# Layer 0 of an eight-layer kernel as one order of steps: attention of later groups, weight making and feed-forward on five engines

## What is computed

```
x = x + _layernorm(_L0_attn_ref(_layernorm(x), Wq, bq, Wk, bk, Wv, bv))
x = x + _layernorm(_L0_ffn_ref(_layernorm(x), gate_w, gate_su, gate_sv, up_w, ..., down_sv))

# attention: for each token alone, 16 queries, 16 keys and 16 values (the 32 heads' queries are summed)
scores = einsum('bsdh,bse->bsde', q, k) * scale;  o = einsum('bsde,bse->bsd', softmax(scores), v)
# feed-forward, 512 -> 1792 -> 512, every weight made from a rank-4 product:
w_eff = w * (su @ sv);  a = x @ gate_eff.T;  b = x @ up_eff.T;  y = (silu(a) * b) @ down_eff.T
```

## Time and profile before

| | us |
|---|---|
| median of 3 runs | 4261.45 |
| lowest and highest | 4254.96, 4264.74 |
| span of the profiled execution | 4243.4 |
| first stage of layer 0 | 0 to 187.9 |
| feed-forward of layer 0 | 187.9 to about 640 |

### The profile page before, as it was taken

How to read it: one execution, slowest core, us unless ns; L and a number is a source line. 1 busy time by engine, 2 the same in 40 slices (tenths; PEclk the granted TensorE clock), 3 DMA queues, 4 the chain that set the end, 5 groups by cost and what they waited for, 6 DMA issues and landing times.

```text
span 4243.4 us, 63398 instructions
## 1 busy us (share of the span) xinstructions
PE 3775.5 (89%) x21648; PEld 1876.8 (44%) x21648; DVE 2793.0 (66%) x4541; ACT 2277.0 (54%) x3947; POOL 1888.5 (45%) x1566
## 2 busy tenths in 40 slices
PE   6799998899888779999999999999999985867899
PEld 2344443223322245555555555555555542443344
DVE  6633235774675468888888888988888866566322
ACT  5522223555456556676666667666676644453222
POOL 5500000000000347787786878777787774462000
PEclk9999997889889989999999999999999997998999
DMA  3100001001100010000000000000000010012100
GB/s 110 54 6 1 0 12 34 1 1 18 35 7 4 10 42 1 24 12 25 13 14 24 1 25 13 25 13 19 18 1 27 4 37 27 23 46 73 31 10 20
DMA packets 62821, 91.36 MB, mean 22 GB/s; under 512 B 12357, under 2 KB 36440, under 8 KB 62500
## 3 DMA queue, kind: packets, MB, share of 16 engines
q1 hardware_dynamic: 61832, 86.72, 7.2%
q10 hardware_dynamic: 672, 0.59, 0.1%
HBM read 73.62 MB, written 6.85 MB: 19 GB/s over the span
## 4 chain that ended last, share of the span: by engine, by line
PE 65%; DVE 15%; issue 8%; ACT 6%; POOL 4%; DMA 1%; SPq 1%; DVEq 0%; POOLq 0%; ACTq 0%
PE psum L329 14%; PE psum L330 14%; PE psum L331 14%; PE psum L1396 3%; DVE arena L1558 3%; PE psum L2499 2%; PE psum L2503 2%; PE psum L1369 2%; PE psum L2491 2%; PE psum L2460 2%; PE psum L1380 2%; ACT xn L218 1%; DVE x L2185 1%; PE psum L2482 1%; PE psum L1365 1%
## 5 line engine op out<-in xcount | busy, mean ns | idle before, releaser
L329 PE MATMUL psum<-xt_hi,arena 128*128 128x512 f16 (+2 forms) x2272 | 872.7, 384 | 31.4 <-DVE arena L531 10.8
L330 PE MATMUL psum<-xt_lo,arena 128*128 128x512 f16 (+2 forms) x2272 | 872.0, 384 | 0.0
L331 PE MATMUL psum<-xt_hi,arena 128*128 128x512 f16 (+2 forms) x2272 | 871.0, 383 | 0.0
L2286 POOL TENSOR_TENSOR arena<-arena 128x1024 f16<-128x1024 f16 x256 | 514.5, 2029 | 50.3 <-DVE arena L2097 33.5
L1314 POOL TENSOR_TENSOR rs<-sd,epsc 128x1 f32<-128x1 f32 x15 | 8.2, 548 | 1087.5 <-DVE sd L1606 1087.5
L329 PE MATMUL psum<-arena 128*128 128x512 f16 (+1 forms) x1152 | 422.4, 370 | 58.3 <-DVE arena L2914 19.0
L1509 ACT ACTIVATE arena<-psum 128x512 f32<-128x512 f32 x576 | 319.7, 598 | 266.3 <-PE psum L1380 176.7
L1558 DVE TENSOR_REDUCE arena<-psum 128x1 f32<-128x512 f32 (+3 forms) x608 | 365.1, 654 | 148.1 <-PE psum L1369 147.1
L330 PE MATMUL psum<-arena 128*128 128x512 f16 (+1 forms) x1152 | 422.2, 370 | 0.0
L331 PE MATMUL psum<-arena 128*128 128x512 f16 (+1 forms) x1152 | 422.1, 370 | 0.0
L329 PEld LDWEIGHTS psum<-xt_hi,arena 128*128 128x128 f16 (+1 forms) x2272 | 224.6, 99 | 280.9 <-issue 16.0
(11 more groups left out here) (338 smaller groups left out, 7882.1 us busy)
## 6 DMA issues: line engine op xcount, KB each, us to landing
arena<-m_wi SPq DMA_DIRECT2D x64, 320.0 KB, 3.0
arena<-m_wo SPq DMA_DIRECT2D x32, 256.0 KB, 2.6
arena<-arena SPq DMA_DIRECT2D x90, 64.0 KB, 2.5
x<-L_attn_x SPq DMA_DIRECT2D x4, 1024.0 KB, 8.3
out<-x SPq DMA_DIRECT2D x4, 1024.0 KB, 4.3
arena<-gate_wT SPq DMA_DIRECT2D x16, 224.0 KB, 2.5
arena<-up_wT SPq DMA_DIRECT2D x16, 224.0 KB, 2.5
arena<-down_wT SPq DMA_DIRECT2D x14, 256.0 KB, 2.6
```

What stands on the lines that cost most here:

```text
L329: nc.tensor.matmul(out, lh, rh, start=start, stop=False)
L330: nc.tensor.matmul(out, lh, rl, start=False, stop=False)
L331: return nc.tensor.matmul(out, ll, rh, start=False, stop=stop)
L2286: nc.gpsimd.tensor_tensor(m4_ar[:, q], heads[q].broadcast_to([P, HG, P]), m4_le.unsqueeze(1).broadcast_to([P, HG, P]), ALU.mult).then_inc( ...
```

## The change

Both stages become one `STEPS0`, walked by `sp_l0`, `pe_l0`, `act_l0`, `dve_l0` and `pool_l0`. Ahead of group 0's products stand only its attention, its "ln" tiles, group 1's "x0" tiles and 16 piece steps. The other 30 piece steps stand two by two after the up products of group 0. The attention of group g+1, its "ln" tiles and the "x0" tiles of group g+2 stand among the blocks of group g; groups 1 to 3 are straight code now. The pieces go by column block (all of gate and up for one fourth of the columns, then the next), and gate f of group 0 waits for the pieces of its own column block. Statistics, scale and power are made for four tiles at once; the square root of these norms is a power on POOL, no longer on ACT. POOL has three `raw1` buffers and multiplies in place. The rank product takes one f16 matmul over 76 rows: rows 0 to 11 hold high x high, 32 to 43 high x low, 64 to 75 low x high of the factors of gate, up and down. For that DVE clears the factor tiles, SP loads each factor three times ahead of all pieces, ACT and DVE convert them. Layer 1's four weight planes are made beside group 1. Not shown: new addresses in the arena, which grows from 34213 to 38100 words of a partition, and a smaller scratch for DMA descriptors.

```diff
-        SEQ0 = [("x0", i) for i in range(3 * GT)]
-        for i in range(GT):
-            SEQ0 += [("ln", i), ("x0", 3 * GT + i)]
-        SEQ0 += [("ln", i) for i in range(GT, NT)]
...
+        for c in range(4):
             for k in range(KT):
-                for c in range(4):
+                for m, (h_, l_) in enumerate(((gh, gl), (uh, ul))):
...
+        def block1(f):
+
+            return 2 * KT * (((f + 1) * P - 1) // QW + 1)
...
+                def batch(n, f):
+                    add(after, f, *[("stat", n + j) for j in range(GT)], ("var", n))
+                    add(after, f + 1, ("scale", n), ("norm", n), ("norm", n + 1))
+                    for j in range(GT):
+                        add(before, f + 2 + j, ("tr", n + j))
+                        add(after, f + 2 + j, ("hi", n + j), ("lo", n + j))
+                        if j + 2 < GT:
+                            add(after, f + 2 + j, ("norm", n + j + 2))
+                if g + 1 < NG:
+                    add(after, 1, ("qkv", g + 1))
+                    for q, part in enumerate(ATTN0[1:]):
+                        add(after, 2 + q, (part, g + 1))
+                    batch(entry0("ln", (g + 1) * GT), 8)
+                if g + 2 < NG:
+                    batch(entry0("x0", (g + 2) * GT), 2)
+                for f in range(F0):
+                    steps.append(("gate", g, f))
+                    if g and f == 1:
+                        steps.append(("carry", g - 1))
+                    steps.extend(before.get(f, []))
+                    steps.append(("up", g, f))
+                    chunk(2)
+                    steps.extend(after.get(f, []))
+                steps.append(("hidden", g))
+                chunk(len(chunks))
+                steps += [("tile", g, j) for j in range(GT)]
...
+            load_x(sp, 0)
+            sp.wait_ge(w1_made, 2)
+            for m, (wide, narrow) in enumerate((("gate_suT", "gate_sv"), ("up_suT", "up_sv"), ("down_sv", "down_suT"))):
+                for part in range(3):
+                    rows = slice(32 * part + RANK * m, 32 * part + RANK * (m + 1))
+                    sp.dma_start(fac_w[rows, :], A[wide]).then_inc(w1_fac, 16)
+                    sp.dma_start(fac_n[rows, m, :], A[narrow]).then_inc(w1_fac, 16)
...
                     if n >= 2:
-                        pe.wait_ge(xt_ok, n - 1)
+                        pe.wait_ge(xt_ok, n - 1 if n < 2 * GT else n)
...
-                nc.tensor.matmul(ps_y[:, i % 2, 0:w], svT[0:RANK, k * P:(k + 1) * P], suT[0:RANK, cols],
+                nc.tensor.matmul(ps_y[:, i % 2, 0:w], fac_nh[0:FR, m, k * P:(k + 1) * P], fac_wh[0:FR, cols],
                                  start=True, stop=True).then_inc(w1_ps, 1)
...
+            for what, n, *f in STEPS0:
+                if what == "factors":
+                    dve.wait_ge(w1_made, 4)
+                    nc.vector.scalar_tensor_tensor(out=fac_wh[64:FR, :], in0=fac_w[64:FR, :], scalar=WS, in1=fac_wh[64:FR, :],
```

More of the change, by code:

```diff
@@ L1090, in pe_front, with pe_l0 @@
+        def pe_l0(pe):
             pe.wait_ge(consts_ok, 5)
-            for what, n in STEPS0:
+            for what, n, *f in STEPS0:
                 if what == "tr":
@@ L1114, in pe_front, with pe_l0_block @@
                             rank(pe, i)
+                elif what in ("gate", "up"):
+                    pe_l0_block(pe, what, n, *f)
+                elif what == "carry":
+                    Tail.pe_x(pe, entry0("tail", n * GT + GT - 1), GT - 1)
+                elif what == "tile":
+                    g, j = n, f[0]
+                    r = g * GT + j
+                    if r >= 2:
+                        pe.wait_ge(y_norm, r - 1)
+                    tok = slice(j * P, (j + 1) * P)
+                    for f in range(F0):
+                        if j == 0:
+                            pe.wait_ge(hid_lo, g * F0 + f + 1)
+                            if g == 0:
+                                if f == 0:
+                                    pe.wait_ge(w1_rk, len(chunks))
+                                pe.wait_ge(w1_lo, GATED1 + f + 1)
+                        last = three(pe, ps_y[:, j % 2, :], hid_h[:, f, tok], hid_l[:, f, tok], dh[:, f, :], dl[:, f, :],
+                                     f == 0, f == F0 - 1)
+                    last.then_inc(y_ready, 1)
+                    if j:
+                        Tail.pe_x(pe, entry0("tail", r - 1), j - 1)
+        def pe_l0_block(pe, what, g, f):
+            i, cols, fc = g * F0 + f, slice(g * GW, (g + 1) * GW), slice(f * P, (f + 1) * P)
+            bank = 2 * (f % 2) + (what == "up")
+            high, low = (gh, gl) if what == "gate" else (uh, ul)
+            if what == "gate":
+                if f == 0:
+                    pe.wait_ge(xt_ok, entry0("ln", g * GT) + GT)
+                if f >= 2:
+                    pe.wait_ge(hid_ok, i - 1)
+                if g == 0:
+                    pe.wait_ge(w1_lo, block1(f))
+            for k in range(KT):
+                last = three(pe, ps_g[:, bank, :], high[:, k, fc], low[:, k, fc], xt_hi[:, k, cols], xt_lo[:, k, cols],
+                             k == 0, k == KT - 1)
+            last.then_inc(gate_ready if what == "gate" else up_ready, 1)
         def rank(pe, i):
@@ L1147, in act_front @@
                     act.wait_ge(a0_w, 2)
[L1148 removed]
+                    nc.scalar.activation(w0h, w0, ACT.Copy, scale=WS).then_inc(a0_w, 1)
                 elif what == "logits":
```

381 lines of the change are left out of this document (247 added, 134 removed).

## The result

The changed kernel takes **4209.65 us** (median of four runs, 4201.33 to 4215.07) against 4258.2 for the kernel before in the same comparison (4250.86 to 4264.74): a ratio of 0.9883, 95% interval 0.9865 to 0.9901, or 48.6 us less. The forecast was 43 us less. The profiled execution spans 4207.6 us and was timed at 4209.37, so only 1.8 us lie around a span.

What follows compares the result with a forecast made beforehand. PE bounds the feed-forward groups (100% busy); the 187.9 us stage ahead is held by small pieces handed round in strict order. 102 - 22 - 16 - 14 - 1 - 6 = 43 us off 4261.5 gives 4218 us, range 4200 to 4238.

Steps and rivals of the forecast that it cites:

- Front, 86 us: Layer 0 ahead of the products: first product at 86 us instead of 187.9, a gain of 102 us.
- New work, 22 us: Rank products, transposes and small matmuls added on PE beside layer 0's products: 22 us (18 to 30).
- Waits, 31 us: PE's waits among layer 0's products: 16 us in group 0, 14 in group 1, 1 in group 2.
- rank 24: Group 0: PE waits for a rank copy standing behind ACT's delayed silu of block 3, 2.8 us.
- tile 15: Group 0: this tile's transposes wait behind DVE's four additions, 8.0 us against 3.0, so 5.0.
- closing: End of group 0: PE waits for the last rank copy before the down products, 3.0 us.
- Clock, 6 us: Groups 0 and 1: granted clock drops at long PE waits, costing 6 us (0 to 12).
- four of my waits are that long: Groups 0 and 1: waits of 2.8 with 2.2, 5.0, 5.6 and 3.5 each cost about 1.5 us of clock.
- The 18 us: Whole kernel before: median about 18 us above the profiled span, carried over unchanged.
- R1: Beside the products: waits mostly vanish as DVE and ACT run ahead, front done at 80; 4186 us, chance 0.22.
- R2: Groups 0 and 1: nine or so waits each drop the clock, 15 + 12 instead of 6; 4239 us, chance 0.20.
- R3: Group 0: the ring of pieces sets the pace, a loss above 4.8 us a piece, 4282 at 5.5; chance 0.08.

Runs made afterwards that it cites:

- experiment 2: Changed kernel with group 0's statistics, norms, planes and small matmuls ahead of the factor conversion, and attention weights loaded before the factors; 4201.8 us, ratio 0.9864.
- experiment 5: Changed kernel with the edits of experiment 1 and experiment 2, plus group 1's x load issued on SP before its first wait for a piece; 4190.09 us.
- experiment 4: Changed kernel with each f16 rank product issued four times; one run, 4205.44 us.
- experiment 1: Changed kernel with high part, low part and next norm ahead of the attention's weights, means and addition in blocks 4 to 7, groups 0 and 1; 4184.32 us.
- experiment 9: Kernel before, unchanged, profiled a second time; span 4248.8 us, layer 0 ending at 631.87.
- experiment 7: Changed kernel with the old piece order, all gate pieces then all up pieces, so 33 piece steps precede the products; one run, 4224.14 us.

## Why the prediction was right

**Front, 86 us: right, in part by luck.** Its steps came where they were forecast. The factors landed at 13.65 us (15.5 forecast), the first statistics began at 21.88 ("near 23"), the first norm at 28.70 ("near 29"), the first additions ended at 68.1 (69) and the first product came at 85.81.

```profile
13.65 1.28 ACT L1236 ACT_TABLE_LOAD   x1 [13.65 <-DMA arena<-down_suT]
...
21.88 0.69 DVE L1320 BATCH_NORM_STATS2 arena<-x 128x6 f32<-128x512 f32 x1
```

Within the first of them four terms were off and about cancelled, which is luck: an issue of a factor took 0.34 us from one to the next, not 0.50, so eighteen cost 6.1 us instead of 9.0; the last factor landed 3.5 us after its issue (10.12 to 13.65), not 2.5; ACT had a table load of 1.28 ahead of its conversions; POOL's power of four columns took 1.03 us, not the 0.55 of one column. What the forecast did not see is that its chain had another beside it of nearly the same length: the statistics at 22 us were on it, yet experiment 2 took them off and gained nothing, because x was late as well and, as far as experiment 5 shows, the pieces.

**New work, 22 us: right.** In group 0 it is 34.2 us (145.4 less 111.2) less 15.7 of waits and 7.1 of clock (0.06 of 118.2), 11.4, where the terms that fall there (31 rank products 6, eight sets of transposes 4, one of small matmuls 2) make 12. There are 29 rank products, not 31, by the order of steps; at the 0.20 us of experiment 4 that is still 6. The 0.2 us was an estimate, and no run shows a rank product's price among dense products by itself: the 0.22 of the earlier trace rows belongs to an f16 matmul of 512 columns, and experiment 4's 0.20 is worked out from group 0's time, waits and clock. The f32 product of before took 1.86 us (x2) in the old front, which are one piece and not two, since line 1124 has 64 records for its 32 pieces. In group 1 it is 21.4 - 10.7 - 5.1 (0.04 of 127) = 5.6, forecast 6; in group 2, 3.0, forecast 4. Together 20.0. These are remainders: an error of 0.6 us in either clock term, from the rounding of the column, would stand in them.

**Waits, 31 us: 26.4.** Place by place, forecast and measured: rank 24 2.8 and 3.08; tile 12 2.2 and 0.52; tile 13 2.1 and 1.88; tile 14 0.8 and 1.62; tile 15 5.0 and 4.37; closing 3.0 and 2.69 with 0.47; one of 1.07 before the second batch was not forecast. Sum 15.7 against 16. Group 1: 5.6 and 4.37, 3.2 and 2.37, 1.2 and 0.33, 3.5 and 2.79, 0.7 and 0.79: 10.65 against 14. Group 2 had none. The walk through DVE's order named the places, and came out 0.7 to 1.2 us too high on each of group 1's first four; whether its gaps between DVE's steps or the product's end were too pessimistic was not tested. For tile 15 the additions were the mis-sized part, 4.17 us and not the 5.5 taken from the earlier trace rows.

**Clock, 6 us: the step that was too small.** The windows give 7.1 and 5.1, 12 us, the upper end of 0 to 12. What failed is less the price than the count. "About 1.5 us each" is near the 1.7 of a single fall (the earlier trace rows have the 0.43 only at the start of the products; behind the wait that ended at 146.86 seven of them followed each other at that step); but "four of my waits are that long" left out the closing wait of group 0 (2.69 us) and tile 25's (2.37), each with a fall of its own, and the wait for rank 24 brought one of twice the length. That is 3.4 + 5 x 1.7 = 11.9. Waits of 1.88 and 1.62 us brought none. Over the two groups a microsecond of waits went with 0.46 us of clock (12.2 of 26.4), much as in experiment 1. In the trace the clock is full where the products are dense (1.00 from 204 to 256) and falls at six of the waits; the measured 12 us are twice the forecast's 6.

**The sum.** 101.9 - 20.0 - 26.4 - 12.2 = 43.3, which closes by itself, since the new work is a remainder. 4.6 too much in waits and 2.0 in work against 6.2 too little in clock: that the total came out to 0.3 us is luck; that the front, the work and the waits came out within their ranges, and the clock at the end of its own, is not. **The 18 us** between span and median were misread in the prediction: 1.8 us lie around a span (4250.58 and 4248.8 in experiment 9), so the profiled execution took about 4245, less than any timed run of that kernel on record (4250.86 to 4271.21). It was a quick one, by 4 us at least in the layers behind layer 0; why stays open. It did no harm, because the sum was a difference. The median fell by 48.6 us, layer 0 by 43.3; the interval of the ratio is 42 to 57 us, so the two agree. The 5.6 us by which the median fell more than the forecast's 43 are no more than the other layers move from one execution to the next.

**The rivals.** R1 (waits vanish): false for this order, since 26.4 us stand in the trace, but experiment 1 shows what it could not know: the work fits between the products if it stands in another order, and 17.3 us come back. Even there 14.2 us of waits remain. R2 (clock, 27 us): right that the clock falls at waits, as at six of them here, wrong in size. It took as much time at the lower level as the waits last and 1.3 us beside for each; the windows show 12 us in all, less than half of its 27. R3 (ring of pieces, slower): false. It begins to lose above 4.8 us a piece; the ring alone can do 2.4 (experiment 7), and beside group 0's products only rank 24 and the last ranks waited for it, 3.08 and 0.47 us. Its one part that may be true is the front of experiment 5.

## What to carry to other kernels

When vector work is put beside dense matrix products, the order of steps on the helping engine decides: put first what the matrix engine waits for next, and the long step behind it (here worth 17.3 us on top of the change's 43). Price a wait with the clock that falls behind it: here 1.7 us at each of five waits (2.37 to 4.37 us) and 3.4 at a sixth, on average half a microsecond for each microsecond of waits. Before a stage is shortened, look on every queue for what stands behind a wait: here a load of x behind a piece kept 6.5 us of what an earlier norm should have brought.

## What the runs showed of the hardware

The additions to x (L1384, two operands in SBUF) took this long for four while POOL multiplied pieces, and while POOL was idle:

```profile
63.87 4.27 DVE L1384 TENSOR_TENSOR x<-x,arena 128x512 f32<-128x512 f32 x4
...
283.68 2.50 DVE L1384 TENSOR_TENSOR x<-x,arena 128x512 f32<-128x512 f32 x4
```

The same four took 5.59 us in the old front. At 141.95 (4.17 us) POOL was busy for 2.85 of the 4.17, at 63.87 for 2.73 of the 4.27, in the old front for 5.29 of the 5.59, and at 283.68 not at all. Above the 2.50 that is 0.6 us for each microsecond of overlap in all three. No run takes POOL away and leaves the rest as it is. The hidden product (L1393), which has one operand in PSUM, kept its time: 691 to 693 ns for each of the 14 of group 0, where POOL was busy for 67 of the 96 us from 93 to 188.6, and 691 to 692 for the 14 of group 3, where POOL had no work. POOL's multiply of a piece was longer beside these additions too, 1.42 us at 144.15 against 2.21 for two at 27.06, where DVE had one step of four columns. And the lower clock mostly comes late: behind the two waits of 4.37 us the 4 us that held most of the wait show 0.96 and 1.00, the next 4 us 0.62 and 0.57; only at rank 24 does it fall before the wait ends (0.69 from 112 to 116).
